# Adding the causal mask of a max pass in the vector engine's reduction instead of in the matmuls, in a decoder layer on one NeuronCore

## What is computed

```python
    k_prev = jnp.concatenate([zero, kc[:, :, :-1]], axis=2)
    kcat = jnp.concatenate([k_prev, kc], axis=3)
    scores = jnp.einsum('bhcqd,bhckd->bhcqk', qc, kcat) / HD ** 0.5
    causal = wq[:, None] + W >= jk[None, :]
    valid = ci[:, None, None] * W + jk[None, None, :] - W >= 0
    mask = causal[None] & valid
    scores = jnp.where(mask[None, None], scores, -jnp.inf)
    attn = jax.nn.softmax(scores, axis=-1)
```

## Time and profile before

| | before |
|---|---|
| median of three runs | 944.12 us (940.3 to 950.16) |
| the profiled execution | 945.94 us, of which the span from first to last instruction is 944.2 us |
| PE busy | 728.0 us (77%), 5008 matmuls |
| DVE busy | 544.3 us (58%), 970 instructions |
| ACT busy | 418.8 us (44%) |
| POOL busy | 192.4 us (20%) |
| granted TensorE clock, mean | 0.866 of full speed |

### The profile page before, as it was taken

The page is one execution under the profiler, slowest core; times in us unless marked ns, Lnnn a source line. Parts: engine busy times, 40 slices in busy tenths (PEclk is TensorE's granted clock), DMA queues, the critical chain, the costliest instruction groups (busy, mean ns, idle before and its releaser), DMA issues.

```text
span 944.2 us, 13998 instructions
## 1 busy us (share of the span) xinstructions
PE 728.0 (77%) x5008; PEld 412.4 (44%) x5008; DVE 544.3 (58%) x970; ACT 418.8 (44%) x610; POOL 192.4 (20%) x231
## 2 busy tenths in 40 slices
PE   3769888888788997989788778689795684468755
PEld 2446455555545443556445443435343221323344
DVE  4378546665854457566465753345652730559977
ACT  3414544434443544643343455132351342169865
POOL 4002121211321202110231031002002000334536
PEclk9968988899998999999898989688797565679979
DMA  8540141504221344151215413130344012000013
GB/s 258 181 134 3 51 134 42 141 14 115 70 82 30 94 104 109 48 150 48 63 47 134 98 41 86 37 108 14 86 108 130 14 40 45 0 1 1 1 45 134
DMA packets 59187, 71.78 MB, mean 76 GB/s; under 512 B 24635, under 2 KB 36079, under 8 KB 59119
## 3 DMA queue, kind: packets, MB, share of 16 engines
q1 hardware_dynamic: 43792, 50.90, 16.8%
q10 hardware_dynamic: 15327, 19.99, 10.6%
HBM read 17.74 MB, written 4.72 MB: 24 GB/s over the span
## 4 chain that ended last, share of the span: by engine, by line
PE 23%; DVE 12%; issue 6%; DMA 6%; ACT 4%; ACTq 4%; POOL 0%; SPq 0%; POOLq 0%; DVEq 0%
PE banks L676 6%; DMA oc<-sums 4%; PE banks L666 4%; ACTq L906 3%; PE banks L623 2%; PE banks L625 2%; PE banks L549 2%; DVE tops L1280 1%; PE banks L720 1%; PE banks L594 1%; DMA sums<-ls 1%; ACT big L882 1%; PE banks L596 1%; PE banks L653 1%; DVE big L1274 1%
## 5 line engine op out<-in xcount | busy, mean ns | idle before, releaser
L1109 DVE TENSOR_REDUCE mneg<-banks 128x4 f32<-128x1024 f32 (+1 forms) x128 | 145.7, 1152 | 73.8 <-PE banks L587 73.2
L1370 POOL TENSOR_SCALAR_AFFINE_SELECT big<-big 128x512 f32<-128x512 f32 x128 | 85.1, 665 | 448.3 <-ACT big L878 446.9
L878 ACT ACTIVATE big<-banks 128x1024 f32<-128x1024 f32 (+1 forms) x128 | 124.1, 973 | 107.1 <-PE banks L616 74.4
L584 PE MATMUL banks<-big 96*128 96x256 bf16 (+1 forms) x512 | 101.6, 296 | 22.2 <-DVE mneg L1109 9.1
L882 ACT ACTIVATE big<-banks 77x1024 f32<-77x1024 f32 x64 | 64.8, 1019 | 110.7 <-PE banks L625 84.6
L549 PE MATMUL banks<-xnT,weights 128*128 128x512 f32 x192 | 91.7, 607 | 3.0 <-DVE big L1082 1.2
L653 PE MATMUL banks<-big 128*17 128x256 f32 (+1 forms) x1152 | 80.1, 371 | 16.8 <-POOL big L1370 16.7
L1113 DVE TENSOR_REDUCE mneg<-banks 128x8 f32<-128x616 f32 x64 | 49.7, 793 | 68.9 <-PE banks L596 68.7
L616 PE MATMUL banks<-big 99*128 99x256 bf16 (+1 forms) x512 | 76.4, 273 | 9.7 <-ACT big L878 5.6
L587 PE MATMUL banks<-causal,identb 128*128 128x256 bf16 x256 | 77.6, 305 | 0.0
L584 PEld LDWEIGHTS banks<-big 96*128 96x128 bf16 x512 | 51.0, 109 | 58.8 <-issue 28.9
(11 more groups left out here) (150 smaller groups left out, 1165.2 us busy)
## 6 DMA issues: line engine op xcount, KB each, us to landing
big<-parts SPq DMA_DIRECT2D x288, 128.0 KB, 2.5
oc<-sums ACTq DMA_DIRECT2D x16, 512.0 KB
oTs<-oe ACTq DMA_DIRECT2D x64, 64.0 KB, 2.7
out_dram<-oTs SPq DMA_DIRECT2D x16, 256.0 KB, 2.1
xs<-in_x_dram SPq DMA_DIRECT2D x3, 1024.0 KB, 10.1
big<-oe ACTq DMA_DIRECT2D x32, 64.0 KB, 2.9
oTx<-oe ACTq DMA_DIRECT2D x32, 64.0 KB, 2.6
big<-kparts SPq DMA_DIRECT2D x96, 9.6 KB, 2.6
```

The source lines that it names most:

```text
L584: e.matmul(bank(p, j)[:, i * 256 + lo * 128:i * 256 + 256], Q[0:96, hh, c * 128:c * 128 + 128], K[0:96, hh, (c - 1 + lo) * 128:(c + 1) * 1 ...
L878: e.activation(pt[u].rearrange("p (i n) -> p i n", i=4)[:, :, 0:n], pair(p).rearrange("p j (s n) -> p (j s) n", s=2)[:, :, 0:n], ACT.Exp, ...
L1109: e.tensor_reduce(M.rearrange("p (h c) -> p h c", h=4)[:, :, c], pair(p).rearrange("p j (s n) -> p (j s) n", s=2)[:, :, lo * 128:256], AX. ...
L1370: e.affine_select(out=P[:, :, 0:128], in_=P[:, :, 0:128], compare_op=ALU.is_ge, fill=0.0, base=0, pattern=[[0, 4], [1, 128]], channel_mult ...
```

## The change

The two identity matmuls of a self-attention max step go: PE issues four matmuls and nothing else. `causal` becomes two tiles of 128 columns, the first all 0 and the second the old triangle. DVE's single `tensor_reduce` per step becomes four `tensor_tensor_reduce` instructions, one per head, each over the head's 256 columns in PSUM (128 for c = 0): it adds `causal`, multiplies by -1, writes the result over the scores in PSUM, and puts the minimum into one column of `mneg`. `d_max` therefore counts 4 per step, and `max_n` computes the count that a waiting step needs. DVE now waits once for POOL's `causal`. `m3t`, the tile between `turnm`'s copy and its DMA, goes from two copies to one, so a copy now waits for the DMA of the half before it. The cross-attention's max steps, the list of steps and the banks are as they were.

```diff
-        causal = sb("causal", [128, 128], BF16)
+        causal = sb("causal", [128, 2, 128], BF16)
...
-        m3t = sb("m3t", [128, 2, 128], BF16)
+        m3t = sb("m3t", [128, 128], BF16)
...
+        def max_n(*s):
+
+            return n_of[s] + 3 * sum(t[1][0] == "s" for t in plan[:at_plan[s] + 1] if t[0] == "max")
...
-                        if n_of[s] == 1:
-                            e.wait_ge(p_set, 4)
-                            e.wait_ge(d_set, 1)
                         lo = 1 if c == 0 else 0
-                        for j in range(2):
-                            for i in range(2):
-                                hh = 2 * j + i
-                                e.matmul(bank(p, j)[:, i * 256 + lo * 128:i * 256 + 256], Q[0:96, hh, c * 128:c * 128 + 128],
-                                         K[0:96, hh, (c - 1 + lo) * 128:(c + 1) * 128], start=(i == 0), stop=False,
-                                         skip_group_check=True)
-                            t = e.matmul(bank(p, j).rearrange("p (s n) -> p s n", s=2)[:, :, 128:256], identb[:, :],
-                                         causal[:, :].rearrange("p (a n) -> p a n", a=1).to_broadcast([128, 2, 128]),
-                                         start=False, stop=True, skip_group_check=True)
+                        for i in range(4):
+                            t = e.matmul(bank(p, i // 2)[:, i % 2 * 256 + lo * 128:i % 2 * 256 + 256],
+                                         Q[0:96, i, c * 128:c * 128 + 128], K[0:96, i, (c - 1 + lo) * 128:(c + 1) * 128],
+                                         start=(i % 2 == 0), stop=True, skip_group_check=True)
...
-                    if AT[job]:
-                        e.wait_ge(land_m[g], 16 * AT[job])
-                    e.copy(m3t[0:96, i, :], bank(p).bitcast(BF16)[0:96, 0:128]).then_inc(a_m3t, 1)
+                    if g:
+                        e.wait_ge(land_m[0], m_landed(job))
+                    elif AT[job]:
+                        e.wait_ge(land_m[1], 16 * AT[job])
+                    e.copy(m3t[0:96, :], bank(p).bitcast(BF16)[0:96, 0:128]).then_inc(a_m3t, 1)
...
-                        e.tensor_reduce(M.rearrange("p (h c) -> p h c", h=4)[:, :, c],
-                                        pair(p).rearrange("p j (s n) -> p (j s) n", s=2)[:, :, lo * 128:256], AX.X, ALU.max,
-                                        negate=True).then_inc(d_max, 1)
+                        if n_of[s] == 1:
+                            e.wait_ge(p_set, 4)
+                        for i in range(4):
+                            S_q = bank(p, i // 2)[:, i % 2 * 256 + lo * 128:i % 2 * 256 + 256]
+                            e.tensor_tensor_reduce(S_q, S_q, causal[:, lo:2, :].rearrange("p a n -> p (a n)"), -1.0, -NEG,
+                                                   ALU.add, ALU.min, M[:, i * NC + c:i * NC + c + 1]).then_inc(d_max, 1)
```

More of the change, by code:

```diff
@@ L378, in build @@
         n_of = count(plan)
+        at_plan = {s: i for i, s in enumerate(plan)}
         at_bank = banks_of(plan, lambda s: 6)
@@ L395, in read_out @@
                     "xkeys": d_xv, "max": d_max, "turnm": a_m3t, "score": a_exp, "out": d_out}[k], {
-                        "turnw": 2 * n, "masks": 2 * n, "keys": 3 * n - 2, "xkeys": 2 * n}.get(k, n)
+                        "turnw": 2 * n, "masks": 2 * n, "max": max_n(*s), "keys": 3 * n - 2, "xkeys": 2 * n}.get(k, n)
+        def max_n(*s):
+            return n_of[s] + 3 * sum(t[1][0] == "s" for t in plan[:at_plan[s] + 1] if t[0] == "max")
         def w_done(s):
@@ L861, in run_scalar @@
                     _, job, g = s
-                    i = rows_n[job, g] % 2
                     e.wait_ge(t_turnm, n_of[s])
-                    if AT[job]:
-                        e.wait_ge(land_m[g], 16 * AT[job])
-                    e.copy(m3t[0:96, i, :], bank(p).bitcast(BF16)[0:96, 0:128]).then_inc(a_m3t, 1)
+                    if g:
[3 more added lines that the diff above has]
+                    e.copy(m3t[0:96, :], bank(p).bitcast(BF16)[0:96, 0:128]).then_inc(a_m3t, 1)
                     e.wait_ge(a_m3t, n_of[s])
-                    e.dma_start(qs[slot(job, g)][96:99, :, :].rearrange("p h t -> p (h t)"), m3t[0:96, i, :]
+                    e.dma_start(qs[slot(job, g)][96:99, :, :].rearrange("p h t -> p (h t)"), m3t[0:96, :]
                                 ).then_inc(land_m[g], 16)
@@ L1119, in run_vector @@
                     M = mneg[:, i, :]
-                    e.wait_ge(d_max, n_of["max", job, g, NC - 1 if job[0] == "s" else NC - 2])
+                    e.wait_ge(d_max, max_n("max", job, g, NC - 1 if job[0] == "s" else NC - 2))
                     if n > 2:
@@ L1336, in run_gpsimd @@
             e.wait_ge(p_set, 3)
-            e.affine_select(out=causal[:], in_=causal[:], compare_op=ALU.is_ge, fill=NEG, base=0,
+            e.affine_select(out=causal[:, 1, :], in_=causal[:, 1, :], compare_op=ALU.is_ge, fill=NEG, base=0,
                             pattern=[[-1, 128]], channel_multiplier=1).then_inc(p_set, 1)
```

## The result

The changed kernel takes 972.06 us (median of four runs, 969.67 to 981.31) against 944.14 (also four runs): 3.1% slower, ratio 1.031 with a 95% interval of 1.022 to 1.040. Measured again it was 1.033 (1.028 to 1.038). The profiled execution took 969.88 us, of which 968.1 are span: 23.9 us more than before's 944.2. The direction and the place were forecast; the size, 62 us, was more than twice too large.

A forecast was written before the change was run, and what follows sets the result against it. PE leads overall; in the 16 max passes PE and DVE form a coupled loop, PE slightly slower, and DVE becomes the bound: 221.8 + 16 x (6.25 + 2.0) = 353.8 against 291.7, +62 us, so 1006 us, range 957 to 1052.

The forecast's parts named there:

- the prediction's own signs of being wrong: Pair distance under 0.40 or over 0.60 us, passes' DVE share under 80%, longer gaps between passes, or a fallen clock.
- a pair: In a max step, one head's big DVE instruction over its columns plus the small one writing 128 x 1; four per step.
- h: DVE's time for one pair in a max step: 0.50 us claimed, 0.42 to 0.58 as bounds.
- The lower bound: h = 0.42 us in the max steps, both instructions overlapping their successor: 0.345 + 0.073; +21 us in all.
- The rival without overlap: DVE's max steps: no instruction overlaps the next, h = 0.58 us or a little more; +103 us, 1047; chance 0.22.
- The row with the 0.08 us: DVE's timeline before: the reduction from 74.67 would end at 75.90, the next starts at 75.82, 0.08 us earlier.
- the idle time that stays: DVE idle time left unfilled in each max pass: 2.0 us, with 1 to 3 as bounds.
- the tie: h near 0.38, or 0.42 with less residual idle time: within 10 us of before; chance 0.06.
- 1.1 from the banks: Max passes: in 22 of 112 later steps PE waits for the first reduction, idling DVE 0.8 us; 1.1 us a pass.
- its two starting waits: Start of each max pass: DVE waits 0.6 us for the first matmuls and mostly a second time; 1.2 us.
- rival 5: The clock falls as PE's busy share in a pass drops from 84% to 60%: +11 us on top, 1017.
- the third rival: Max passes: DVE's idle time takes its added work, so up to 32 us of PE's come back: 914; chance 0.04.

The follow-up runs named there:

- e2b: The changed kernel with two identity matmuls per max step put back, adding a tile of zeros, second measurement: 965.63 us, ratio 1.0245 to the kernel before.
- e1: The kernel before with the 256 mask matmuls taken out, causal mask left out of the max pass, DVE's reduction unchanged: 950.59 us, ratio 1.0093.
- e5: The changed kernel with each of the four DVE instructions cut to the triangle's 128 columns: 947.81 us, ratio 1.0038 to the kernel before.

## Why the prediction was right or wrong

**Right.** The max passes are where the time goes and the rest keeps its length (from the end of the last pass 391.6 us before, 390.1 after). DVE takes the lead in them: 84% busy, against a forecast of over 85. PE's waits for `mneg` went from 9.1 to 21.1 us. Taking out the mask matmuls brought nothing. DVE's waits for the max step's matmuls fell, but from 73.2 to 53.1 us and not to under 40, since 41 of them stand ahead of the passes. Of the prediction's own signs of being wrong two came: a pair's distance under 0.40 us, and a fallen clock. The single `m3t` cost nothing to be seen: no wait of ACT for that DMA is among the waits.

**Wrong: the price of a pair, the largest term.** h was 0.50 us, with 0.42 and 0.58 as its bounds, and is 0.38. The big instruction was sized well by its neighbour (0.425 estimated, 0.46 measured, 0.38 to its successor). The step that failed is the argument that the small one "reads what the big one has only when its last element is through", so that the big one keeps its full duration and 0.073 us of the small one is added. Measured, the big one overlaps what follows by 0.08 us, and the small one adds nothing, since the next big one starts with it. DVE's added work is 45.9 / 16 = 2.9 us a pass, not 6.25. That is 54 us of the sum. The lower bound too was wrong, because it still charged 0.073 us for the small one. The rival without overlap falls. Beside it stood the rule of the Trainium skill, page "VectorE: DVE Perf Modes", section "The DRAIN you can't avoid", that the next DVE operation does not start until the pipeline is empty. The same section says that a next operation that is not held starts earlier; the prediction left that out, and the 0.38 us between instructions of 0.46 agree with it. The row with the 0.08 us pointed the right way and not far enough.

**Wrong: the idle time that stays.** 2.0 us a pass was assumed, with 1 to 3 as bounds, and it is 3.3: 20 us of the sum, in the other direction. With the true h and 2.0 us the sum would have been 16 x (2.87 + 2.0) - 69.9 = +8, near the tie. The prediction added up only waits for the max step's matmuls: 1.2 us at the start and 1.1 from the banks, cut to 2.0. Those it had too large: the runs show 12.0 us in the 16 passes, 0.75 a pass. The 73.2 us in the earlier trace rows misled it, since 45 of them stand before the first reductions, outside the windows, and so does the first of its two starting waits. What it left out is larger. DVE's queue is in order, and inside the passes it waits 28.5 us for ACT's part of the `qk` steps before and 30.9 after, 1.9 a pass. Part of that is the clock's: with the mask matmuls' PE work restored DVE's added work fills 6 us of it, and the whole idle time is 2.7 us a pass (e2b). So about 0.6 a pass, 8 to 10 us, was the clock's; e1 against before gives 8 us by another way.

**Wrong in kind: rival 5.** The clock was treated as 11 us on top, as a consequence of a DVE-bound pass. The size was near. But it does not need the longer DVE step: e1 pays it with DVE unchanged. And "up to 32 us come back", the third rival's prize, did not come where its condition was met: e1, with DVE's work as before, and e5, with less, are both slower than before. Whether a still faster DVE would win it back was not tested.

**The sum as it came out,** by exact windows: 45.9 us of DVE work, less 17.6 us of idle time filled, less 4.5 us outside the passes: 23.9 us in the profiled executions.

**Open.** Whether the clock is all that holds e5 at 948 us; and what the passes would gain if the `qk` waits went, since their size (28.5 us before, 22.2 in e2b) was read from the traces and no run took them away. Nor did a run part the write over the scores in PSUM, the four signals of `d_max` and the single `m3t` from the rest of DVE's half; the first two are inside the 0.38 us, and for the third there is only the absence of a wait.

## What to carry to other kernels

Look at the granted clock before you take matmuls off PE: where they keep its clock up, their removal can cost more than they did, and a test that removes them alone shows it in one run. Price a chain of small vector instructions by the distance between starts, and test it before you argue about which one can overlap; a sum of durations would have been 0.60 us here, and the distance is 0.38. When an engine's idle time is to absorb new work, split it by what ended it and take only what lies in the stretch in question: here the waits for PE shrank by 16 us, and those for ACT, a third engine, grew by 2, since the clock fell.

## What the runs showed of the hardware

- The accumulator's read-out behind a `tensor_tensor_reduce` has a row of 0.14 us of its own and starts together with the next instruction of the chain; heads of 256 columns stood 0.38 us apart and heads of 128 columns 0.25.
- Useless matmuls can shorten a kernel: 256 of them in the max passes took the ratio from 1.0093 to 1.0019, and fillers in PE's waits took 1.1% off the kernel before. At the last projection 12 fillers that ended 10.2 us before it left its first six groups at 1.2 GHz, and 52 that ended 1.2 us before it had it at 2.4 GHz; number and distance were changed together.
- Removed matmuls left PE's busy time in the passes nearly where it was (244.4 and 243.2 us), since what remained ran at half clock more often: the passes' mean clock went from 0.93 to 0.83.
- A lower TensorE clock made DVE idle by way of ACT: DVE's waits for ACT's part of the `qk` steps in the passes were 28.5 us at a mean clock of 0.93 and 39.0 at 0.83 with DVE's work the same, and 22.2 at 0.92 and 30.9 at 0.81 with the longer DVE step. Within each of these pairs PE's own work differs by the mask matmuls, and the lower clock goes with less of it.
